# 32-head attention: the stacks filled by ScalarE, the head halves moved inside SBUF to every fourth partition, and TensorE's waits placed inside the groups

## The reference

```python
q = (x @ Wq).reshape(b, n, 32, 8)              # x is the layer norm of the running x
k, v = jnp.split(ctx @ Wkv, 2, axis=-1)        # both (b, 256, 32, 8)
q = apply_axial_rope(q, pos_map)
k = apply_axial_rope(k, ctx_pos_map)
logits = jnp.einsum('bqhd,bkhd->bhqk', q, k) / np.sqrt(8)
w = jax.nn.softmax(logits, axis=-1)
attn = jnp.einsum('bhqk,bkhd->bqhd', w, v)
return attn.reshape(b, n, 256) @ Wout + bout
```

## Time and profile before

| | |
|---|---|
| median of 3 runs | 1067.77 us (1067.21 to 1071.0) |
| profiled execution | 1065.51 us |
| its span in the trace | 1063.3 us |
| mean granted TensorE clock | 0.868 |
| busy, share of the span: PE, DVE, ACT, POOL | 78%, 67%, 36%, 41% |
| preparation of this attention, end of the previous block to the first scores | 588 to 646 us |
| loop over heads | 646 to about 799 us |

### The profile page before, as it was taken

How to read it: one execution, slowest core, us unless ns; L and a number is a source line. 1 busy time by engine, 2 the same in 40 slices (tenths; PEclk the granted TensorE clock), 3 DMA queues, 4 the chain that set the end, 5 groups by cost and what they waited for, 6 DMA issues and landing times.

```text
span 1063.3 us, 12926 instructions
## 1 busy us (share of the span) xinstructions
PE 826.6 (78%) x4202; PEld 519.1 (49%) x4202; DVE 710.4 (67%) x1136; ACT 377.5 (36%) x822; POOL 430.7 (41%) x297
## 2 busy tenths in 40 slices
PE   5797888740988988887498465799884896979993
PEld 2232333340767766665487233454443585645661
DVE  5988999788988888888655843577854646422222
ACT  1523322240444343433455101465560541203331
POOL 4006666101576666665088600332530141142331
PEclk8987888855999999999699685899996997789997
DMA  5103223480122112220100333312215101042114
GB/s 202 44 1 119 79 75 137 183 290 12 40 80 80 66 54 79 79 79 0 70 1 1 69 67 53 126 35 96 71 54 211 31 1 60 11 165 93 45 46 148
DMA packets 28674, 83.77 MB, mean 79 GB/s; under 512 B 3376, under 2 KB 17216, under 8 KB 27104
## 3 DMA queue, kind: packets, MB, share of 16 engines
q1 hardware_dynamic: 26224, 75.35, 21.9%
q0 software_dynamic: 2256, 6.18, 1.6%
q10 hardware_dynamic: 144, 1.57, 0.4%
HBM read 67.74 MB, written 19.45 MB: 82 GB/s over the span
## 4 chain that ended last, share of the span: by engine, by line
PE 43%; DVE 19%; issue 15%; POOL 11%; DMA 5%; ACT 5%; SPq 1%; DVEq 0%; POOLq 0%; ACTq 0%
PE ps L1682 6%; PE ps L512 6%; POOL M L675 4%; PE ps L1328 4%; PE ps L391 3%; PE ps L505 3%; PE ps L895 3%; DVE M L644 2%; DVE Z L314 2%; POOL ZT L978 2%; PE ps L1347 2%; DVE M L652 2%; ACT N L1753 2%; PE ps L1724 1%; POOL slot_scratch L1213 1%
## 5 line engine op out<-in xcount | busy, mean ns | idle before, releaser
L783 PE MATMUL ps<-W,F 128*128 128x256 f32 x544 | 150.9, 402 | 53.6 <-POOL F L738 30.7
L783 PEld LDWEIGHTS ps<-W,F 128*128 128x128 f32 x544 | 101.8, 197 | 86.6 <-DVE W L851 42.3
L586 POOL TENSOR_TENSOR M<-M 128x1024 f32<-128x1024 f32 x32 | 75.3, 2354 | 94.4 <-DVE M L466 53.6
L682 POOL TENSOR_TENSOR W<-W,M 128x1024 f32<-128x1024 f32 x32 | 75.3, 2355 | 84.6 <-DVE M L652 84.6
L1753 ACT ACTIVATE N<-ps 128x512 f32<-128x512 f32 x128 | 69.5, 594 | 105.1 <-PE ps L1686 105.1
L1682 PE MATMUL ps<-M,W 32*128 32x256 f32 x512 | 78.0, 436 | 35.0 <-DMA W<-rot_scratch 16.5
L1774 DVE TENSOR_REDUCE W<-ps 128x4 f32<-128x1024 f32 x64 | 78.1, 1221 | 23.2 <-PE ps L1682 15.9
L644 DVE TENSOR_TENSOR_SCAN M<-ps,M 128x512 f32<-128x512 f32 x64 | 78.0, 1219 | 21.4 <-POOL M L675 21.4
L815 ACT ACTIVATE F<-ps 128x128 f32<-128x128 f32 x136 | 37.8, 278 | 149.8 <-PE ps L783 149.8
L770 PE MATMUL ps<-W,F 128*128 128x256 f32 x272 | 83.2, 389 | 0.0
L1682 PEld LDWEIGHTS ps<-M,W 32*128 32x128 f32 x512 | 49.1, 203 | 65.9 <-issue 38.2
(11 more groups left out here) (279 smaller groups left out, 1724.5 us busy)
## 6 DMA issues: line engine op xcount, KB each, us to landing
M<-dbl_scratch SPq DMA_DIRECT2D x48, 512.0 KB, 3.9
W<-in_gu SPq DMA_DIRECT2D x1, 4800.0 KB, 16.3
W<-in_gu SPq DMA_DIRECT2D x1, 4352.0 KB, 13.9
att_scratch<-W SPq DMA_DIRECT2D x32, 128.0 KB
slot_scratch<-in_slots SPq DMA_DIRECT2D x1, 3999.0 KB, 18.4
M<-slot_scratch SPq DMA_DIRECT2D x3, 1032.0 KB, 9.4
W<-in_gu SPq DMA_DIRECT2D x2, 1536.0 KB, 6.8
W<-in_dn SPq DMA_DIRECT2D x1, 2176.0 KB, 18.6
```

Of the source, the lines that this page charges most:

```text
L586: nc.gpsimd.tensor_tensor(dBu[:, t, :], du[0][:, t, :], Bb[:, par, :], ALU.mult).then_inc(S("dBu_rdy"), 1)
L682: nc.gpsimd.tensor_tensor(u[1][:, t, :], u[1][:, t, :], hC[:, t, :], ALU.add).then_inc(S("y1_acc"), 1)
L783: last = nc.tensor.matmul(up, ztt[:, par, c, :], gu[:, c, s, :], start=(c == 0), stop=(c == DC - 1))
```

## The change

Four edits, all in the third attention:

- The two fills move from GpSimd to ScalarE. `attn2_scalar_ones` writes `kst` with a Copy of a column of ones, broadcast over 8192 elements, after `x_done` and ahead of the copies of the values; `attn2_scalar_clear` writes `qst` the same way with scale 0, behind the copies of the layer norm's transposes and ahead of the exponentials.
- `rot_scratch` and its four writes and waits go. Each rotated half moves by four transfers from `rot` to the stack, inside SBUF, and the 8 dims now land in partitions 32*b, 32*b+4, ..., 32*b+28. The maximum takes row 1.
- Since the transfers now read `rot` itself, rotations 2 and 3 wait until all four transfers of the keys' half (`stack0`, `stack1`) have landed; before, they waited for the write to DRAM.
- In `group` the waits for `qmax_rdy` of head e and for `e_done` move from ahead of the whole group to ahead of the first `turned` that needs them, and each `turned` waits for its own bank alone.

```diff
@@ rotate
             if x >= 2:
-                dve.wait_ge(S(f"rot_out{c}"), 16)
+                dve.wait_ge(S(f"stack{c}"), 16 * BATCH)
@@ new functions
+        def attn2_scalar_ones(act):
+            act.wait_ge(S("x_done"), 2 * NT)
+            nc.scalar.activation(kst.rearrange("p h n -> p (h n)"), col("ones")[:, 0:1].to_broadcast([P, HEADS * SEQ]),
+                                 ACT.Copy).then_inc(S("keys_ones"), 1)
+
+        def attn2_scalar_clear(act):
+            nc.scalar.activation(qst.rearrange("p h n -> p (h n)"), col("ones")[:, 0:1].to_broadcast([P, HEADS * SEQ]),
+                                 ACT.Copy, scale=0.0).then_inc(S("queries_clear"), 1)
@@ attn2_stacks_sync
                 sp.wait_ge(S("rot_rdy"), x + 1)
-                sp.dma_start(rot_dram[x], rot[:, c, :]).then_inc(S(f"rot_out{c}"), 16)
-                sp.wait_ge(S(f"rot_out{c}"), 16 * (x // 2 + 1))
                 if x in (0, 2):
                     sp.wait_ge(S("keys_ones") if x == 0 else S("queries_clear"), 1)
-                src = rot_dram[x].rearrange("(d h) (b n) -> b d h n", d=HD, b=BATCH)
                 for b in range(BATCH):
-                    sp.dma_start(stack[32 * b:32 * b + HD, 16 * c:16 * (c + 1), :], src[b]).then_inc(S(f"stack{x}"), 16)
+                    sp.dma_start(stack[32 * b:32 * b + 32:4, 16 * c:16 * (c + 1), :],
+                                 rot[:, c, b * SEQ:(b + 1) * SEQ]).then_inc(S(f"stack{x}"), 16)
@@ attn2_gpsimd
-            nc.gpsimd.memset(kst, 1.0).then_inc(S("keys_ones"), 1)
-            nc.gpsimd.memset(qst, 0.0).then_inc(S("queries_clear"), 1)
@@ group
-                if e >= 0:
-                    pe.wait_ge(S("qmax_rdy"), e + 1)
-                    if 4 * e + 2 * which - 1 > 0:
-                        pe.wait_ge(S("e_done"), 4 * e + 2 * which - 1)
                 for half in range(2):
                     for i in range(2):
                         if h < HEADS:
                             last = scores(h, own[i], half)
                     for i in range(2):
                         if e >= 0:
+                            if half == i == 0:
+                                pe.wait_ge(S("qmax_rdy"), e + 1)
+                            if half == 0 and 4 * e + 2 * which + i >= 3:
+                                pe.wait_ge(S("e_done"), 4 * e + 2 * which + i - 2)
                             last = turned(e, other[i], half, 4 * e + 2 * which + i)
@@ attn2_vector
-            spots = negmax.rearrange("p q (b m) -> p b q m", b=BATCH)[:, :, :, HD]
+            spots = negmax.rearrange("p q (b m) -> p b q m", b=BATCH)[:, :, :, 1]
@@ scalar block
             angles_scalar(act)
+            attn2_scalar_ones(act)
             attn2_scalar_values(act)
             ln_scalar(act, 4, 2)
+            attn2_scalar_clear(act)
             attn2_scalar(act)
```

More of the change, by code:

```diff
@@ L234, in flamingo @@
         assert m.at <= HEADS * TOK // 2
-        rot_dram = [nc.dram_tensor(f"rot_scratch{x}", (P, TOK), F32, kind="Internal").ap() for x in range(4)]
         attU = M[:, 0:2 * TOK].rearrange("p (c n) -> p c n", c=DC)
```

## The result

The changed kernel takes 1044.09 us (median of 4 runs, 1041.89 to 1044.75) against 1069.38 for the kernel before in the runs beside it; the ratio is 0.977 (95% interval 0.975 to 0.980). The medians are 25.3 us apart; 25.0 were forecast. By its own value the forecast was 1042.8 us, with a range of 1036 to 1049.

What follows compares the result with a forecast made beforehand. Waits, not a busy engine, were taken to bound the attention's preparation. 12.4 us from the fills and 12.6 from the transfers, 0 from the groups' waits and the clock, gave 1067.8 - 25.0 = 1042.8 us, range 1036 to 1049.

Steps and rivals of the forecast that it cites:

- The layer norm: Third attention's preparation: GpSimd's fills block VectorE's layer-norm steps; moving them ends the transposes at 599.8 instead of 612.2, 12.4 us earlier.
- ScalarE's fills: Preparation: each fill of 8192 elements takes 7.3 us on ScalarE, bounds 6 and 14, and costs nothing on the chain.
- Rival 3: Preparation: ScalarE's fills take 14 us each, the queries' stack lands at 626.6, gain 19.2 us, time 1048.6; chance 0.07.
- The transfers: Ahead of the first scores: stack moves at 176 GB/s, lands some 5 us after issue, hidden; 12.6 us gained.
- The step that carried it: Stack transfers: neither 1 KB pieces nor engines hold the rate at 62 GB/s; the 8 neighbouring target partitions do.
- The waits: Loop's groups: the second `turned` still sets group A's end, period stays 3.99 us; gain 0, bounds 0.05 per head either way.
- The clock in the loop: Loop's start: TensorE's clock falls again as the first two heads are sparse; 0 of up to 5.3 us gained.
- The sum: Preparation: first scores start at 620.9 instead of 645.86, 25.0 us earlier, 12.4 from the fills and 12.6 from the transfers.

## Why the prediction was right

**The layer norm.** Forecast: released by the fills' move, 12.4 us. Shown: the steps take 2.67 us in the changed kernel and with the fills alone, 14.29 with the moves alone, 7.43 with one fill back. The release itself is right, and that the fills are the cause was argued before and is now shown. The size was 1.1 us too large: from the first step to the end of the transposes it took 603.97 - 599.66 = 4.3 us, not 3.5, and the keys' projection 3.87, not 3.43. In both TensorE ran in part at the low clock (0.55 from 602 to 605), while I had taken the pace of a block with the clock at 1.00. The earlier trace rows had the transposes of this very block at 3.83 us, with the clock at 0.50, which I passed over. Here TensorE stood for only 1.65 us ahead of the transposes; that the clock could fall there was not in the sum.

**ScalarE's fills.** Forecast 7.3 us each, hidden. They took 7.04 and 7.02; the values' copies ended at 600.9 and the transposes' first result was ready only after that. The clear was over at 611.5, the queries' stack issued at 618.5. Rival 3 is out.

**The transfers.** Forecast: 176 GB/s, landed about 5 us after the issue, hidden below 6.9. Shown: 162 GB/s, and the scores wait for VectorE. The step that carried it, reading from the earlier trace rows that neither 1 KB pieces nor 8 engines hold the rate and so the target partitions do, is confirmed by the neighbouring targets at 60 GB/s. Of the two pages of the Trainium skill that I had set against each other, the port map of "SBUF — State Buffer", section "Door 1: The DMA port swizzle", is the one that this case bears out, in its direction: the neighbours' 60 GB/s stand near the 54 of two ports. The 162 are well below what eight ports would give at the 27 GB/s of the Trainium skill (an estimate of 216), so with the spread something else limits, which no run here shows. The engine count of the Trainium skill, "DMA: Bandwidth & Descriptors", section "Why a DMA increments its semaphore by 16 and not by 1", is not denied: the share of 0.50 of 16 engines fits 8 at work. It is just not what tells the two rates apart.

**The waits.** Forecast 0 with bounds of 0.05 us per head either way, by the argument that the second `turned` alone sets group A's end. The period fell by 0.05, the bound on the saving side. The argument missed that the two groups answer differently: 0.10 saved in A, 0.06 lost in B. The conclusion for the time, nothing that can be measured, holds.

**The clock in the loop.** Forecast: falls again, 0 of 5.3 us gained. It did (head 2 at 17.1 us after the start, 17.25 before), and the run with 9 matmuls shows that the price was right: 5.7 us over the three heads. The reason given was only half of it. I had laid the fall to the sparse first heads, but it came at 625.2, 3.6 us after TensorE stopped and ahead of the first scores; the run with 4 matmuls shows that it can fall in the sparse heads too, with hardly a standstill before them.

**The sum.** Against the preparation of before, 23.9 came of 25.0; the miss is the 1.1 us at the low clock. That the medians are 25.3 apart is in part luck: single executions of one kernel differ by 3 us and more here, and the kernel before had medians of 1065.35 to 1067.6 in the three later sets of runs, against the 1069.38 of this one.

## What to carry to other kernels

Look for what GpSimd runs when a VectorE step takes many times its usual duration, and move long GpSimd fills and sums away from VectorE's TENSOR_SCALAR steps, the two kinds that were held here (the layer norm's and the masking). ScalarE filled 128 x 8192 in 7.0 us, and the VectorE steps beside it kept their times (1.23 us for each step of a rotation); what waited was ScalarE's own next work, and here nothing hung on it. When a transfer into few partitions is slow, compare its rate per engine with another of the same piece size before blaming either, and try partitions that lie four apart. Taking a wait away shows the next one behind it: the load at head 3 hid a block by GpSimd, and only both together gave 8 us.

## What the runs showed of the hardware

- VectorE's layer-norm steps (TENSOR_SCALAR, SBUF to SBUF) are held by a GpSimd fill until it ends: 14.3 us beside two fills, 7.43 beside one, 2.67 beside none. A sum of two SBUF operands on VectorE took its usual 1.22 us beside the same fill.
- A VectorE bitwise step on 128 x 1536 int32 is held by GpSimd's float32 addition of two SBUF operands: 5.20 us instead of 0.96. Two of VectorE's reductions, which read PSUM, took 2.36 us together beside the same addition in the kernel with the bias early, as they do in the changed kernel without it.
- A transfer of 1 KB pieces into 8 neighbouring partitions moved at 60 to 62 GB/s, from DRAM and from SBUF alike; into 8 partitions that lie four apart it moved at 162.
- TensorE's clock fell during the layer norm's transposes (0.55) after a standstill of only 1.65 us. It stayed at 1.00 through two heads with half of the matmuls when 9 more matmuls (7.8 us) ran directly behind the projections and up to the loop, but not when 4 (3.5 us) did. At the start of the loop of the changed kernel it took some 20 us of work to rise again, at heads that each took 5 to 6 us instead of 3.9. What decides between the two lengths stays open.
- Waits that are already satisfied cost TensorE about 0.06 us more per group in the middle of a group of small matmuls than at its start: the period is 3.94 us with group B's waits inside and 3.87 to 3.88 with them ahead.
